# First batch of a gated block: carries tile by tile, diag(D) on VectorE, y to x2 interleaved, GpSimd pausing

## The chip, the cores and the metric

The kernel runs on one core of a Trainium2 chip. The metric is the device time of one execution in microseconds (us), the median of three runs. The engines are named as in the profile: PE is TensorE (matrix products and transposes), PEld its weight loads, DVE is VectorE, ACT is ScalarE, POOL is GpSimd, SP is the engine that only issues DMAs here.

## The reference

Four batches of 512 rows by 512 columns go through two parts. The first is a state space model (Mamba) over a context of 256 columns, gated by the normalised input; the second is a mixture of experts with one shared and seven routed experts.

```python
def _ssm_forward(hidden_states, z, in_proj_w, conv_w, conv_b, x_proj_w, dt_proj_w, dt_proj_b, A_log, D):
    x = jnp.einsum('ed,bld->bel', in_proj_w, hidden_states)
    ...
    u = jax.nn.silu(xc + conv_b[None, :, None])          # xc: causal convolution of x, 4 taps
    x_dbl = jnp.einsum('ke,bel->bkl', x_proj_w, u)       # dt_lo, Bm, Cm
    delta = jax.nn.softplus(jnp.einsum('er,brl->bel', dt_proj_w, dt_lo) + dt_proj_b[None, :, None])
    # scan over l, 16 states:  state = state * exp(delta * A) + (delta * u) * Bm ;  y = sum_n state * Cm
    y = y + D[None, :, None] * u
    y = y * jax.nn.silu(z)
    return jnp.swapaxes(y, 1, 2)

x = x + jnp.tanh(g_xattn[0]) * ssm(ctx, layernorm(x))
x = x + jnp.tanh(g_ffn[0]) * moe(layernorm(x))           # silu(x@W1) * (x@Wg) @ W2, 1 shared + top 3 of 7
```

## The kernel before

A batch is four tiles of 128 rows or channels by 512 (T = 4). The products of the experts are made in three passes from a high and a low half of each operand (`x_hi`, `x_lo`, `w_split`, `h_hi`, `h_lo`), 12 products of 128x512 for one bank.

Each engine has its own program, written out by hand in its order; the engines meet at semaphores. There is no planner: what stands earlier in an engine's program is done earlier, and an instruction that waits holds up all behind it on that engine.

The first batch's state space part is done by itself, since there are no expert products yet to lie beside it:

- **The front.** The context is projected (`in_proj`), convolved (`first_conv`), and `xproj` gives `dt_x` and `xdbl`. The softplus of delta is built on ACT and DVE: ACT reads the product of a tile twice and takes an exponential (`front_dt`, three instructions per tile into `dA[0]` and `delta`), and later the logarithm into `st[0]` (`front_ln`). DVE computes the rounding error of 1 + e in three instructions per tile (`front_carry`: L1238, L1241, L1246, all in `st[1]` and `delta`), and adds the logarithm (`front_delta`, L1253). Then it makes delta times u (`front_du`, L1264), which also waits until PE has used `u` for the term D u (`first_init`, L589, which reads `diag_D`, four diagonal matrices). POOL normalises the input of z in place meanwhile (L1668).
- **The scans.** For each of 16 states DVE multiplies (`bmul`, L1275) and scans (`scan`, L1284), two instructions each; PE transposes the states into rows, ACT scales them by C, PE adds them into four PSUM banks (`first_add`, L596). PE also projects the contexts of the later batches in halves (`in_proj`, L550), and ACT stages them to memory (`stage`).
- **From y to x2.** DVE makes y from bank and gate (`first_make_y`, L1337), adds the residual (L1353), takes the statistics (L1356), and `first_mean_and_var` and `first_x2` (L1331) make the normalised x2. POOL makes the low halves of the shared expert's three matrices here (`first_low`, L1596, four instructions for each matrix) and the two powers for the norm (`first_power`, L1588). PE makes 20 products that nobody reads, to keep its clock up (`keep_warm`, L533), and then transposes x2 (`x2_to_columns`, L631); ACT makes `x_hi` from it and DVE `x_lo`.
- **The shared expert of batch 0** (`shared_step`), with the front of batch 1 laid between its products at numbered places g (PE), j (ACT) and p (DVE). DVE does 8 instructions of the convolution of batch 1 (L1179) before the first `h_tmp` (L1444) and 4 behind it. ACT's `front_silu` (L858) waits for these, and behind it stands ACT's `router_columns` (L984), which PE's `router_rows` waits for at g = 3.

Of the kernel before, what the change touches and what calls it, by code (L numbers as in the profile page):

```python
# [28 lines left out]
def gated_block(nc, t, out):  # L29
# [22 lines left out]
    with ExitStack() as ctx:  # L52
# [88 lines left out]
        setup_a = sem("setup_a")  # L141
        ctx_ld = sem("ctx_ld")
# [380 lines left out]
        def _(pe):  # L523
# [212 lines left out]
            def shared_step(b, m=None):  # L736

                def between(g):
                    if g == 1:
                        router_columns(b)  # L740
                    if g == 3:
                        router_rows(b)
                    if m is not None:
                        names = {5: ("xproj", "init0"), 6: ("dt0", "init1"), 7: ("dt1", "ccols"), 8: ("dt2", "init2"),
                                 9: ("dt3", "init3"), 10: ("z0", "z1")}.get(g, ())
                        front(m, *[name for name in names if name in front_names(m)])
# [38 lines left out]
            pe.wait_ge(setup_a, 2 + T)  # L785
# [6 lines left out]
            for n in range(DS):  # L792
# [9 lines left out]
                in_proj(2 + q // T, q % T, (n % 2,))  # L802
# [17 lines left out]
        def _(act):  # L820
# [311 lines left out]
            for et in range(T):  # L1132
                act.activation(diag_D[:, et, :], ident[:], ACT.Copy, scale=D_col[:, et:et + 1]).then_inc(setup_a, 1)
            for et in range(T):
                front_dt(0, et)
            front_ccols(0)
            front_ln(0, range(T))
# [7 lines left out]
            for n in range(DS):  # L1145
                decays(0, T * (n + 2), T * (n + 2) + 2)
                for i in range(T):
                    first_scale(n, i)
# [4 lines left out]
                if n % 2:  # L1153
                    stage(2 + q // T, q % T)
                if n == DS - 2:
# [14 lines left out]
        def _(dve):  # L1170
# [176 lines left out]

            def residual(m, tiles):

                dve.wait_ge(xres_ld, 16 * (m + 1))  # L1350
                for i in tiles:
                    dve.wait_ge(y_ready, T * m + i + 1)
                    dve.tensor_tensor(x1[:, i, :], y_rows[:, i, :], x_rows[:, i, :], ALU.add).then_inc(x1_ready, 1)  # L1353
                for i in tiles:
                    dve.wait_ge(x1_ready, T * m + i + 1)
                    dve.bn_stats(bn[:, i, :], x1[:, i, :]).then_inc(x2stat, 1)  # L1356
# [121 lines left out]
            front_carry(0, (0, 1))  # L1478
            front_carry(0, (2, 3))
# [15 lines left out]
            for h in range(2):  # L1495
                for i in (2 * h, 2 * h + 1):
                    first_make_y(i)
                    residual(0, (i,))
                first_mean_and_var(h)
# [80 lines left out]
        def _(pool):  # L1580
# [91 lines left out]
            first_low(1, (0, 1))  # L1672
            first_power(0)
            first_low(1, (2,))
            first_power(1)
            first_low(1, (3,))
# [43 lines left out]
```

## Time and profile before

| | us |
|---|---|
| median of 3 runs | 1354.61 (1353.84 to 1354.89) |
| profiled execution, its own time | 1356.03 |
| its span in the profile | 1354.2 |
| PE busy | 1307.6 (97%) |
| DVE busy | 963.6 (71%) |
| ACT busy | 622.5 (46%) |
| POOL busy | 613.8 (45%) |

The profile is of one execution. In the page's 40 slices PE stands at 9 tenths or more except in the first, the second and the fifth (7, 8 and 7 tenths; a slice is 33.9 us). PE's mean granted clock over the execution is 0.991 of 2.4 GHz. Times are counted from the start of the span. The row of a merged group gives its start, the time to the end of its last instruction, and the number of instructions (x4); fp32 products show as two records each.

### The profile page before, as it was taken

The page shows a single profiled execution, that of the slowest core. Times are in us where ns is not written, and L with a number is a line of the kernel's source. Part 1 is how long each engine was busy: PE and PEld are TensorE (multiplying, and loading weights), DVE is VectorE, ACT ScalarE, POOL GpSimd, SP SyncE. Part 2 cuts the span into 40 slices and gives each one's busy share as a digit, 9 for nine tenths or more (in the row PEclk, how much of TensorE's full clock was granted, in tenths as well). Part 3 has the DMA queues.
Part 4 walks back from the last instruction along what each step waited for, and adds up shares of the span by engine and source line. Part 5 has one row for each costly group of instructions (what it writes and reads, how often), then busy time and mean ns, then how long its engine had stood idle before and what let it go on. Part 6 is the DMA issues. An engine that isn't in the chain of part 4 may idle for free.

```text
span 1354.2 us, 17537 instructions
## 1 busy us (share of the span) xinstructions
PE 1307.6 (97%) x5986; PEld 1032.5 (76%) x5986; DVE 963.6 (71%) x1062; ACT 622.5 (46%) x1016; POOL 613.8 (45%) x337
## 2 busy tenths in 40 slices
PE   7899799999999999999999999999999999999999
PEld 4455478787777787888887878888887888888887
DVE  6999867899999776699999776699999623111111
ACT  6888466665565336544454135555444121111111
POOL 3000545788898521467667511566767411111111
PEclk8999899999999999999999999999999999999999
DMA  6211676776667755555566755655555665555552
GB/s 224 78 63 55 228 285 248 270 260 234 222 251 272 286 201 192 197 171 174 196 210 210 278 189 202 202 190 184 176 183 189 218 218 187 186 186 186 186 191 88
DMA packets 92588, 269.69 MB, mean 199 GB/s; under 512 B 11664, under 2 KB 11792, under 8 KB 92128
## 3 DMA queue, kind: packets, MB, share of 16 engines
q1 hardware_dynamic: 87200, 261.54, 55.9%
q10 hardware_dynamic: 5312, 7.16, 1.5%
q8 instruction: 45, 0.74, 0.2%
q14 instruction: 31, 0.25, 0.1%
HBM read 210.73 MB, written 57.93 MB: 198 GB/s over the span
## 4 chain that ended last, share of the span: by engine, by line
PE 80%; DVE 13%; issue 4%; ACT 2%; DMA 0%; DVEq 0%; POOL 0%; ACTq 0%
PE ps_hg L527 24%; PE ps_h L527 21%; PE ps_y L527 15%; PE ps_y L708 8%; DVE st L1284 7%; PE ps_mid L606 5%; DVE y_rows L1295 1%; DVE st L1275 1%; PE ps_h L596 1%; PE ps_mid L568 1%; ACT dA L937 1%; PE ps_y L550 1%; PE ps_mid L527 1%; PE ps_hg L596 1%; PE ps_y L596 1%
## 5 line engine op out<-in xcount | busy, mean ns | idle before, releaser
L1606 POOL TENSOR_TENSOR h_lo<-h_tmp,h_hi 128x512 fp32r<-128x512 f32 x128 | 237.1, 1856 | 478.2 <-ACT h_hi L1012 415.8
L527 PE MATMUL ps_h<-x_hi,w_split 128*128 128x512 f32 x1024 | 344.9, 399 | 1.1 <-ACT x_hi L974 0.9
L527 PE MATMUL ps_hg<-x_hi,wg_split 128*128 128x512 f32 x1024 | 342.8, 396 | 0.6 <-DVE h_tmp L1444 0.6
L1284 DVE TENSOR_TENSOR_SCAN st<-dA,st 128x1024 f32<-128x1024 f32 x128 | 326.9, 2564 | 0.0
L1444 DVE TENSOR_TENSOR h_tmp<-h_tmp,ps_hg 128x512 f32<-128x512 f32 x128 | 88.0, 688 | 267.1 <-PE ps_hg L527 264.6
L527 PE MATMUL ps_y<-w_split,h_hi 128*128 128x512 f32 x1024 | 254.1, 395 | 0.0
L1012 ACT ACTIVATE h_hi<-h_tmp 128x512 fp32r<-128x512 f32 x128 | 80.7, 630 | 328.9 <-DVE h_tmp L1444 328.9
L527 PEld LDWEIGHTS ps_h<-x_hi,w_split 128*128 128x128 f32 x1024 | 193.2, 189 | 42.4 <-issue 2.5
L527 PEld LDWEIGHTS ps_hg<-x_hi,wg_split 128*128 128x128 f32 x1024 | 192.4, 188 | 40.6 <-issue 1.0
L527 PEld LDWEIGHTS ps_y<-w_split,h_hi 128*128 128x128 f32 x1024 | 188.5, 188 | 37.9
L1006 ACT ACTIVATE h_tmp<-ps_h 128x512 f32<-128x512 f32 x128 | 76.2, 595 | 283.1 <-PE ps_h L527 280.1
L527 PE MATMUL ps_hg<-x_lo,wg_split 128*128 128x512 f32 x512 | 199.5, 390 | 0.0
L527 PE MATMUL ps_h<-x_lo,w_split 128*128 128x512 f32 x508 | 197.9, 390 | 0.0
L1275 DVE TENSOR_TENSOR st<-u,b_all 128x1024 f32<-128x1024 f32 x128 | 188.2, 1480 | 0.1
L937 ACT ACTIVATE dA<-delta,neg_A 128x511 f32<-128x511 f32 x256 | 162.8, 708 | 5.6 <-DVE dA L1225 2.8
L606 PEld LDWEIGHTS ps_mid<-ident,st 128*128 128x128 f32 x748 | 90.0, 140 | 58.2 <-DVE st L1284 21.4
L708 PE MATMUL ps_y<-w_split,h_lo 128*128 128x512 f32 x512 | 134.3, 393 | 0.0
L606 PE MATMUL ps_mid<-ident,st 128*128 128x128 f32 x748 | 112.0, 275 | 20.8 <-DVE st L1284 20.8
L1437 DVE SCALAR_TENSOR_TENSOR acc<-ps_y,coef,acc 128x512 f32<-128x512 f32 x112 | 82.5, 737 | 69.5 <-PE ps_y L708 69.5
L1627 POOL TENSOR_TENSOR st<-st,wg_raw 128x512 f32<-128x512 f32 x48 | 96.4, 2031 | 47.1 <-DVE st L1284 47.1
L527 PEld LDWEIGHTS ps_hg<-x_lo,wg_split 128*128 128x128 f32 x512 | 96.5, 188 | 18.7
L708 PEld LDWEIGHTS ps_y<-w_split,h_lo 128*128 128x128 f32 x512 | 94.6, 188 | 20.8 <-POOL h_lo L1606 1.7
(163 smaller groups left out, 1329.0 us busy)
## 6 DMA issues: line engine op xcount, KB each, us to landing
w_split<-split_scratch SPq DMA_DIRECT2D x192, 512.0 KB, 5.2
wg_split<-split_scratch SPq DMA_DIRECT2D x96, 512.0 KB, 4.6
split_scratch<-w_split SPq DMA_DIRECT2D x64, 512.0 KB, 4.3
b_all<-xd_scratch SPq DMA_DIRECT2D x64, 256.0 KB, 4.1
split_scratch<-wg_split SPq DMA_DIRECT2D x32, 512.0 KB, 3.1
w_raw<-in_W_dram SPq DMA_DIRECT2D x14, 1024.0 KB, 8.1
wg_raw<-in_Wg_dram SPq DMA_DIRECT2D x7, 1024.0 KB, 9.5
dA<-in_x_dram SPq DMA_DIRECT2D x4, 1024.0 KB, 7.4
```

Source lines behind the costliest of these rows:

```text
L527: mm = pe.matmul(out_, lhs[a], rhs[c], start=first and q == 0, stop=last and q == len(sides) - 1)
L606: mm = pe.transpose(ps_mid[bank][:, et * P:(et + 1) * P], st[n % 2][:, et, i * P:(i + 1) * P], ident[:])
L708: mm = pe.matmul(ps_y[i % 3][:], h_lo[:, j, i * P:(i + 1) * P], half(2, j, 0), start=False, stop=j == T - 1)
L937: act.activation(dA[odd][:, et, 1:L], delta[:, et, 1:L], ACT.Exp, scale=neg_A[:, et, n:n + 1]).then_inc(da_ready, 1)
L1006: act.activation(h_tmp[j % 2][:], ps_h1[j % 2][:], ACT.Silu).then_inc(t_done, 1)
L1012: act.activation(h_hi[:, j, :], h_tmp[j % 2][:], ACT.Copy).then_inc(hh_ready, 1)
L1275: dve.tensor_tensor(st[odd][:, two], u[:, two], b_all[odd][:].rearrange("p (a l) -> p a l", a=1).broadcast_to([P, 2, L]), ALU.mult).then_i ...
L1284: dve.tensor_tensor_scan(flat[1], flat[0], flat[1], 0.0, ALU.mult, ALU.add).then_inc(scan_done, 1)
L1437: dve.scalar_tensor_tensor(out=acc[:, i, :], in0=ps_y[i % 3][:], scalar=scale, in1=before[:, i, :], op0=ALU.mult, op1=ALU.add).then_inc(ac ...
L1444: dve.tensor_tensor(h_tmp[j % 2][:], h_tmp[j % 2][:], ps_hg[:], ALU.mult).then_inc(h_made, 1)
L1606: pool.tensor_tensor(h_lo[:, j, :], h_tmp[j % 2][:], h_hi[:, j, :].bitcast(F32), ALU.subtract).then_inc(hl_ready, 1)
L1627: pool.tensor_tensor(st[odd][:, et, :], st[odd][:, et, :], c_all[used % 2], ALU.mult).then_inc(col_scaled, 1)
```

## The change

Seven edits, all in the first batch or in the shared step beside it:

1. `diag_D` is made by DVE (four instructions, before the carries) in place of ACT; PE waits for a semaphore of its own (`diag_made`).
2. `front_carry` of batch 0 is done tile by tile in place of pair by pair.
3. ACT does `front_ln` of batch 0 ahead of `front_ccols`.
4. The last half of `in_proj` for batch 3 goes from state 15 to state 14, where the last tile is now projected in one piece; its staging on ACT goes with it, to before the fourth scaling of state 14. The load of ACT's table for Silu goes to the end of state 13.
5. On DVE, y, residual and statistics of the tiles are interleaved, so that most instructions have another one between them and the one that they depend on.
6. POOL does no low halves between the first matrix (`first_low(0)`) and the end of x2: it does the two powers and then waits for all four tiles of x2.
7. In the shared step of batch 0, PE transposes the columns of C for batch 1 (`ccols`, L579) behind the first half of the down products (g = 8) in place of before it (g = 7).

The 20 warming products stay as they are.

```diff
@@ shared_step (PE)
+                        if not late(m):
+                            names = {7: ("dt1",), 8: ("ccols", "dt2", "init2")}.get(g, names)
                         front(m, *[name for name in names if name in front_names(m)])
@@ tensor
-            pe.wait_ge(setup_a, 2 + T)
+            pe.wait_ge(diag_made, T)
...
-                in_proj(2 + q // T, q % T, (n % 2,))
+                if n < DS - 2:
+                    in_proj(2 + q // T, q % T, (n % 2,))
+                elif n == DS - 2:
+                    in_proj(2 + q // T, q % T)
@@ scalar
-            for et in range(T):
-                act.activation(diag_D[:, et, :], ident[:], ACT.Copy, scale=D_col[:, et:et + 1]).then_inc(setup_a, 1)
             for et in range(T):
                 front_dt(0, et)
+            front_ln(0, range(T))
             front_ccols(0)
-            front_ln(0, range(T))
...
+                    if n == DS - 2 and i == T - 1:
+                        stage(NB - 1, T - 1)
                     first_scale(n, i)
...
-                if n % 2:
+                if n % 2 and n < DS - 2:
                     stage(2 + q // T, q % T)
+                if n == DS - 3:
+                    table(ACT.Silu)
@@ vector
-            front_carry(0, (0, 1))
-            front_carry(0, (2, 3))
+            for et in range(T):
+                dve.tensor_scalar(diag_D[:, et, :], ident[:], D_col[:, et:et + 1], None, ALU.mult).then_inc(diag_made, 1)
+            for et in range(T):
+                front_carry(0, (et,))
...
             for h in range(2):
-                for i in (2 * h, 2 * h + 1):
-                    first_make_y(i)
-                    residual(0, (i,))
-                first_mean_and_var(h)
+                first_make_y(2 * h)
+                if h:
+                    first_mean_and_var(0)
+                residual_add(0, 2 * h)
+                first_make_y(2 * h + 1)
+                residual_stats(0, 2 * h)
+                residual_add(0, 2 * h + 1)
+                residual_stats(0, 2 * h + 1)
+            first_mean_and_var(1)
@@ gpsimd
             first_low(0, range(T))
-            first_low(1, (0, 1))
             first_power(0)
-            first_low(1, (2,))
             first_power(1)
-            first_low(1, (3,))
+            pool.wait_ge(x2_ready, T)
+            first_low(1, range(T))
             first_low(2, range(T))
```

How the instructions stand, first on DVE at the front of batch 0. Before, where `st` and `dA` are the buffers of 1 + e and e, and `delta` takes the correction:

```order
L1476 TENSOR_SCALAR neg_A<-neg_A 128x64
L1238 TENSOR_SCALAR st<-dA 128x512 x2
L1241 SCALAR_TENSOR_TENSOR st<-st,dA 128x512 x2
L1246 TENSOR_TENSOR delta<-delta,st 128x512 x2
L1238 TENSOR_SCALAR st<-dA 128x512 x2
```

And after:

```order
L1491 TENSOR_SCALAR neg_A<-neg_A 128x64
L1494 TENSOR_SCALAR diag_D<-ident,D_col 128x128 x4
L1246 TENSOR_SCALAR st<-dA 128x512
L1249 SCALAR_TENSOR_TENSOR st<-st,dA 128x512
L1254 TENSOR_TENSOR delta<-delta,st 128x512
L1246 TENSOR_SCALAR st<-dA 128x512
```

Four small instructions stand ahead of the carries, and a tile's three instructions follow each other.

POOL between the z of batch 0 (`dA`) and the low half of the shared step's first `h_tmp`, before. `w_split` stands for the first matrix at the top and the third lower down, `wg_split` for the second, `rstd` for the powers:

```order
L1668 TENSOR_SCALAR dA<-dA,mv,rstd 128x512 x4
L1596 TENSOR_TENSOR w_split<-w_raw,w_split 128x512 x4
L1596 TENSOR_TENSOR wg_split<-wg_raw,wg_split 128x512 x2
L1588 TENSOR_TENSOR rstd<-var_eps,minus_half 128x2
L1596 TENSOR_TENSOR wg_split<-wg_raw,wg_split 128x512
L1588 TENSOR_TENSOR rstd<-var_eps,minus_half 128x2
L1596 TENSOR_TENSOR wg_split<-wg_raw,wg_split 128x512
L1596 TENSOR_TENSOR w_split<-w_raw,w_split 128x512 x4
L1601 TENSOR_TENSOR w_split<-w_raw,w_split 128x512
L1606 TENSOR_TENSOR h_lo<-h_tmp,h_hi 128x512
```

And after:

```order
L1690 TENSOR_SCALAR dA<-dA,mv,rstd 128x512 x4
L1618 TENSOR_TENSOR w_split<-w_raw,w_split 128x512 x4
L1610 TENSOR_TENSOR rstd<-var_eps,minus_half 128x2 x2
L1618 TENSOR_TENSOR wg_split<-wg_raw,wg_split 128x512 x4
L1618 TENSOR_TENSOR w_split<-w_raw,w_split 128x512 x4
L1623 TENSOR_TENSOR w_split<-w_raw,w_split 128x512
L1628 TENSOR_TENSOR h_lo<-h_tmp,h_hi 128x512
```

All eight low halves of the second and third matrix now stand behind both powers; before, three stood ahead of the second power.

PE at the end of the shared step's gate products, before (`dt_x` is batch 1's dt product, `xdbl` its C columns, `h_hi` the down products):

```order
L575 MATMUL ps_mid<-dt_x,dt_w 128x512
L579 MATMUL ps_mid<-ident,xdbl 128x128 x4
L527 MATMUL ps_y<-w_split,h_hi 128x512 x16
L575 MATMUL ps_mid<-dt_x,dt_w 128x512
L572 MATMUL ps_mid<-ident,st 128x128 x4
```

And after:

```order
L576 MATMUL ps_mid<-dt_x,dt_w 128x512
L528 MATMUL ps_y<-w_split,h_hi 128x512 x16
L580 MATMUL ps_mid<-ident,xdbl 128x128 x4
L576 MATMUL ps_mid<-dt_x,dt_w 128x512
L573 MATMUL ps_mid<-ident,st 128x128 x4
```

The four transposes, which wait until ACT has read a bank, have gone behind 16 products that don't.

## Rows read from the trace of the kernel before

**Rows 1.** Busy time in stretches: us, each engine, PEclk, DMA share, GB/s.

```profile
38.90:145.20 106.30, 97.65 (x402) 54.86 (x402) 106.29 (x65) 89.28 (x150) 0.00 (x0) 0.98 0.24 82
145.20:166.90 21.70, 15.04 (x62) 10.24 (x63) 17.41 (x28) 7.15 (x13) 15.76 (x13) 0.82 0.64 226
182.60:1354.20 1171.60, 1149.01 (x5369) 937.24 (x5366) 801.22 (x907) 491.67 (x798) 579.77 (x311) 1.00 0.60 207
```

**Rows 2.** The timeline of ACT at the front: start us, us, instruction, count.

```profile
22.59 1.26 ACT L1133 ACTIVATE diag_D<-ident,D_col 128x128 f32<-128x128 f32 x4
23.76 0.67 ACT L916 ACTIVATE dA<-ps_mid,dt_b 128x512 f32<-128x512 f32 x1
...
29.88 0.66 ACT L919 ACTIVATE dA<-dA 128x512 f32<-128x512 f32 x1
...
31.96 2.56 ACT L928 ACTIVATE st<-dA,ones 128x512 f32<-128x512 f32 x4
```

**Rows 3.** The timeline of DVE at the front.

```profile
23.47 0.19 DVE L1476 TENSOR_SCALAR neg_A<-neg_A 128x64 f32<-128x64 f32 x1
25.62 0.43 DVE L1238 TENSOR_SCALAR st<-dA 128x512 f32<-128x512 f32 x1 [1.97 <-ACT dA L919]
...
31.06 1.28 DVE L1241 SCALAR_TENSOR_TENSOR st<-st,dA 128x512 f32<-128x512 f32 x2
...
33.47 2.90 DVE L1253 TENSOR_TENSOR delta<-delta,st 128x512 f32<-128x512 f32 x4
...
36.51 2.29 DVE L1264 TENSOR_TENSOR u<-delta,u 128x2048 f32<-128x2048 f32 x1
```

**Rows 4.** The timeline of POOL at the front.

```profile
24.54 10.79 POOL L1668 TENSOR_SCALAR dA<-dA,mv,rstd 128x512 f32<-128x512 f32 x4
```

**Rows 5.** The timeline of PE at the front.

```profile
33.56 1.06 PE L589 MATMUL ps_y<-diag_D,u 128*128 128x128 f32 x8
```

**Rows 6.** The timeline of PE at the end of the scans.

```profile
146.61 1.02 PE L550 MATMUL ps_y<-acc,in_w 128*128 128x512 f32 x2
147.47 1.02 PE L596 MATMUL ps_h<-y_rows,ident 128*128 128x512 f32 x2
...
150.95 5.15 PE L533 MATMUL ps_y<-gw 128*128 128x512 f32 x20
```

**Rows 7.** The timeline of DVE from y to x2.

```profile
149.47 1.32 DVE L1353 TENSOR_TENSOR z<-y_rows,delta 128x512 f32<-128x512 f32 x1
...
159.02 0.69 DVE L1353 TENSOR_TENSOR z<-y_rows,delta 128x512 f32<-128x512 f32 x1
...
160.84 4.02 DVE L1331 TENSOR_SCALAR st<-z,mv,rstd 128x512 f32<-128x512 f32 x4
```

**Rows 8.** The timeline of POOL from the last scan on.

```profile
145.28 4.96 POOL L1596 TENSOR_TENSOR w_split<-w_raw,w_split 128x512 fp32r<-128x512 f32 x4 [109.95 <-DVE st L1284]
```

**Rows 9.** Busy time in the stretch between the warming products and x2.

```profile
156.10:161.40 5.30, 0.00 (x0) 0.00 (x0) 5.05 (x11) 0.00 (x0) 1.28 (x2) 0.76 0.89 290
```

**Rows 10.** The chain that ended last, at the first expert products: start us, us, what.

```profile
166.92 3.75 PE ps_h L527 x8
...
177.15 2.75 PE ps_h L527 x12
```

**Rows 11.** The timeline of DVE, the convolution of batch 1.

```profile
167.40 6.24 DVE L1179 SCALAR_TENSOR_TENSOR u<-dA,conv_w,u 128x509 f32<-128x509 f32 x8
...
176.00 4.82 DVE L1179 SCALAR_TENSOR_TENSOR u<-dA,conv_w,u 128x511 f32<-128x511 f32 x4
```

**Rows 12.** The timeline of POOL beside it.

```profile
178.52 1.75 POOL L1612 TENSOR_TENSOR wg_split<-wg_raw,wg_split 128x512 fp32r<-128x512 f32 x1
```

**Rows 13.** The timeline of ACT, the router's columns.

```profile
181.39 0.57 ACT L984 ACTIVATE xdbl<-ps_mid 14x512 f32<-14x512 f32 x1
```

**Rows 14.** Waits of PE from 182 us on: waited for, us in total, times, longest.

```profile
PE ps_mid L606 <- DVE st L1284: 17.3, 21, 1.7
PE ps_mid L579 <- ACT y_rows L893: 1.1, 1, 1.1
```

More of the change, by code:

```diff
@@ L141, in gated_block @@
         setup_a = sem("setup_a")
+        diag_made = sem("diag_made")
         ctx_ld = sem("ctx_ld")
@@ L1346, in make_y, with residual_add, residual_stats @@
                                              in1=z2[:, i, :], op0=ALU.mult, op1=ALU.mult).then_inc(y_ready, 1)
+            def residual_add(m, i):
+                dve.wait_ge(xres_ld, 16 * (m + 1))
+                dve.wait_ge(y_ready, T * m + i + 1)
+                dve.tensor_tensor(x1[:, i, :], y_rows[:, i, :], x_rows[:, i, :], ALU.add).then_inc(x1_ready, 1)
+            def residual_stats(m, i):
+                dve.wait_ge(x1_ready, T * m + i + 1)
+                dve.bn_stats(bn[:, i, :], x1[:, i, :]).then_inc(x2stat, 1)
             def residual(m, tiles):
-                dve.wait_ge(xres_ld, 16 * (m + 1))
                 for i in tiles:
-                    dve.wait_ge(y_ready, T * m + i + 1)
-                    dve.tensor_tensor(x1[:, i, :], y_rows[:, i, :], x_rows[:, i, :], ALU.add).then_inc(x1_ready, 1)
+                    residual_add(m, i)
                 for i in tiles:
-                    dve.wait_ge(x1_ready, T * m + i + 1)
-                    dve.bn_stats(bn[:, i, :], x1[:, i, :]).then_inc(x2stat, 1)
+                    residual_stats(m, i)
             def make_x2(m):
```

## The prediction

> **What bounds the kernel now.** I first read the table of stretches, to see which engine carries which part. The reader is to see three stages. In the scans of batch 0, DVE is busy for 106.29 of 106.30 us [rows 1]: whatever lets them start earlier ends them earlier by as much. From the last scan to the first expert product, 21.7 us, no engine is full: DVE has 17.41, POOL 15.76, PE 15.04, and this is a chain through DVE. From 182.6 us on PE is busy for 1149.0 of 1171.6 us [rows 1], and DVE, which waits for PE in each step, follows it, so a gain made before is kept to the end; the 17.3 us in 21 waits for scans [rows 14] move along with it. The change touches only the first 210 us. Then I read the timelines of each engine there: the front up to 36.5 us, the way from y to x2, and the first expert step.
>
> **The front, edits 1 to 3.** Before, ACT makes diag_D from 22.59 and begins the first tile's dt at 23.76 [rows 2]; without it, all that follows on ACT comes 1.17 earlier, and the last e is ready at 30.54 - 1.17 = 29.4. The tiles' e come 1.66 apart (the fourth exponential starts at 29.88, the first at 23.76 + 0.57 + 0.57), the first is ready at 24.4. With `front_ln` ahead of `ccols` (about 0.25) the logarithms gain that too: they end at 34.52 - 1.42 = 33.1.
>
> DVE gets four 128x128 instructions behind neg_A, which ends at 23.66 [rows 3]. The trace has no such instruction; the nearest row is neg_A itself, half as wide, 0.19, and the other end is the 128x512 of the same kind, 0.43. I take 0.19 each, so 0.76 and the carries may start at 24.4, just when the first e is there; with 0.43 each they would start at 25.4, one us late. Then each tile takes 0.43 + 0.04 for the first instruction, 0.64 + 0.08 for the second because its result is waited for, and 0.60 for the third (1.28 for two, from rows 3): 1.79. DVE is a little slower than ACT's 1.66, so the fourth tile's carries end at 24.4 + 3 x 1.79 + 0.47 + 0.72 + 0.60 = 31.6, where before they ended at 33.47 [rows 3]. The four additions take 2.4 and the clearing of one column 0.8 with its wait, so delta u starts at 34.2 in place of 36.51. In the trace two instructions beside POOL's normalisation took 0.4 longer than their kind (the four additions 2.90 in place of 2.5 [rows 3]); since DVE has no slack now, both count, and I take 0.6 for them: 34.8, a gain of **1.7**. The ends are 1.0 (0.43 for each diag, and clashes as well) and 2.3 (neither). What might be late next: PE's term D u, which ended at 34.6 [rows 5], is moved with ACT's reading of the banks (1.17 earlier) and is at 33.4 to 34.5, so it just does not bind; z of batch 0 comes from POOL (done at 35.33, [rows 4]) and is wanted by the second state, some 8 us later.
>
> This is a place to weigh a page. The rows show DVE's TENSOR_SCALAR of 0.43 at 25.62 in the midst of POOL's four TENSOR_SCALARs of 2.7 each (10.79 / 4) [rows 3, 4], not held up by them. The Trainium skill (SBUF — State Buffer, Who interferes with whom) says that a VectorE instruction in a two-port mode, which tensor_scalar can take, and a GpSimd one exclude each other for a whole instruction. By that the four diag instructions or the first carry would wait for POOL's power or first tile; the trace disagrees for this pair of instructions. It is the fourth rival below.
>
> **State 14 and 15, edit 4.** At state 15 the half projection (0.86, from 146.61 to 147.47, [rows 6]) goes from ahead of the first sum. At state 14 the same 0.86 comes in; PE is not quite full there (97.65 of 106.30 in the scans, [rows 1]), and I estimate that about half of it is hidden and the rest pushes the transposes of state 15: the first sum starts at 147.05 in place of 147.47. So y of tile 0 comes 0.4 earlier. The table load of 1.28 on ACT is in ACT's gaps in either place. But then the residual (L1353) of tile 0, which took 1.32 from 149.47 where the free one takes 0.69 [rows 7], ended when POOL's fourth low half (4 in 4.96 from 145.28, so to 150.24, [rows 8]) had ended, plus 0.55. That does not move: **0** from edit 4, unless DVE asks before POOL's fourth one starts at 149.0 (I have DVE at 149.05); the third rival.
>
> **From y to x2, edits 5 and 6.** The other residuals pay the same clash: it is one POOL instruction, then one of DVE, in turn. Interleaved and with POOL silent, I lay the sequence out from 150.8: y1, statistics 0, add 1, statistics 1 (0.66, 0.61, then 0.73 where the next depends), y2 at 153.4, mean and variance 0.37, add 2 at 154.5, y3, statistics 2, add 3 at 156.3, statistics 3, variance, x2 from 158.2 against 160.84 [rows 7]. The second power takes about 0.9 after that, and the last two x2 at 0.43 end at 160.1; before, the four took 4.02 [rows 7] and ended at 164.86. So x2 is ready 4.8 us earlier. PE's transposes then follow at 158.7, after 3.1 us of idleness; before it was 5.3, and the clock went from 1.0 to 0.5 within (mean 0.76) [rows 9]. I take it that it falls again; then PE needs to 162.6 for the transposes, and the first product starts at 163.4 in place of 166.92 [rows 10].
>
> **What that gives back.** POOL now has eight low halves to do from 160.15, at 1.23 each, and the first weight split of the next step behind them; before, five were left at 161.9 and they were nearly through when DVE's convolution of batch 1 began at 167.40. That first one waited, the other seven went at 0.66 [rows 11]. Now it begins at 163.9, with one of POOL's eight under way and four to come, and the split behind them. Both read two tensors from SBUF, so they take turns: in the second convolution group four took 4.82 against two POOL instructions of 1.75 [rows 11, 12], which is 1.19 for POOL's and 0.55 for DVE's, 1.74 a pair. The first ends at 165.6, the sixth at 174.3, the eighth at 175.6; `h_tmp` of the first tile comes at 175.65, where it was 175.39. Behind it the four of the last tap meet the same two POOL instructions as before, then ACT's silu, then `router_columns`: read to the end at 182.2 (before 181.96, [rows 13]). PE's `router_rows` then starts at 182.25 in place of 182.65. Of 3.5 us that PE was earlier, only **0.4** is left, and PE stands idle for 3 us from 179.2. The bounds: -1.5 (pairs at 2.0, below) and 3.5 (no turns).
>
> The Trainium skill (the same page and section) gives the same rule, an exclusive lock between a VectorE op with two SBUF inputs and a GpSimd op that reads SBUF; it speaks against edit 6, since pausing only moves the low halves into the convolution. Here the trace agrees (0.69 free, 1.32 beside POOL).
>
> **Edit 7.** PE waited 1.1 us at g = 7 for ACT to read a bank [rows 14]. Behind 16 products the bank has long been read. ACT's reading of the columns comes at about the time that ACT gets there anyway, but PE's second init transposes may wait some 0.25 for it. Gain **0.85**, between 0.5 and 1.1.
>
> **The sum.** 1.7 + 0 + 0.4 + 0.85 = 2.95 us. The profiled execution took 1356.03 (span 1354.2 and 1.8 around it), and would take 1353.1; the median of the runs is 1.4 lower, 1354.61, and I predict 1351.7 for it.
>
> **Rivals.**
> - *The clock falls a second time.* In the 3 us before `router_rows` (and perhaps before the second gate products) PE does nothing; before, 5.3 us of that took the clock down from 1.0 (2.4 GHz) to 0.5 (1.2 GHz) [rows 9]. Then the next products run at 1.2 GHz: 8 took 3.75 where 12 take 2.75 [rows 10], so 0.24 lost on each; ten of them give 2.4. Time: 1351.7 + 2.4 = 1354.1. For it: the idle stretch is as long as the one ahead of x2. Against it: PE is full on both sides of it. The Trainium skill (TensorE: Matmul & The Clock Gate, the section on the HAM clock gate) says that the count of slow products differs from run to run of one kernel; no run here shows it.
> - *The backlog costs more than it brings.* If DVE and POOL take turns at their full lengths (1.27 and 0.74, 2.0 a pair in place of 1.74), the eight convolution instructions end 2.1 later, `router_rows` at 184.4 in place of 182.65: 1.8 lost in place of 0.4 gained. PE then idles for 5 us, so the clock falls too, 2.9 (the 12 products of a bank at half speed). -1.7 + 1.8 + 2.9 - 0.85 = 2.1 slower: 1356.7, and 1357.4 with the front at its low end. It decides when `h_tmp` of the first tile comes behind 177. Against it: the pairs of 1.74 in rows 11 and 12.
> - *DVE gets ahead of POOL's fourth low half.* Then the residual of tile 0 ends 1.2 earlier, x2 and all the turns with it: 1350.5. It takes 0.1 us.
> - *The diag instructions are blocked by POOL.* The carries would start when the first of POOL's 2.7 us has ended, 27.3 in place of 24.4, and lose 2.8: 1354.5. Against it, rows 3 and 4.
> - *The convolution doesn't take turns with the low halves.* Then all 3.5 us are kept: 1351.7 - 3.1 = 1348.6. Against it, rows 11.
>
> **Chances.** The forecast 0.42; the second fall of the clock 0.22; the costly backlog 0.10; DVE ahead 0.12; diag blocked 0.06; no turns 0.08. What a measurement of this kernel can tell from no change is 0.2%, 2.7 us, so faster means under 1351.9. The forecast lies just at it, and about six tenths of it is beyond; with the third and the fifth rival and a little of the first this makes 0.47 faster, 0.43 the same, 0.10 slower. The range is 1349.4 to 1356.0: it leaves out most of the fifth rival and of the second.
>
> **What would show it.** Delta u at 34.8 (34.2 to 35.5), and the last scan's end at about 143.5. The last x2 near 158.4 (4.8 before its old place, and 1.7 on top), the first convolution instructions at 1.7 us each beside POOL, the first `h_tmp` later than the end of its gate products, and a wait of PE of about 3 us at `router_rows`. No wait at L580 for an `init` bank. I am wrong if the convolution goes at 0.66 each, if PE has no such wait, or if the scans start less than 1 us earlier. A clock of 0.5 behind `router_rows` shows the first rival.

## The result and the profile after

The changed kernel takes 1357.85 us (median of 15 runs, 1356.61 to 1359.72), the kernel before in the same rounds 1355.47 (15 runs). The ratio is 1.0020, 95% interval 1.0014 to 1.0027: 2.7 us slower by the ratio, where 3 us faster was forecast. The profiled execution took 1359.72 (span 1357.9), 3.69 us of span more than the one before; it was the slowest of the 15, so part of what this profile shows is not in the median.

The front, ACT. Columns: start us, us, instruction, count.

```profile
22.65 0.26 ACT L1137 ACTIVATE neg_A<-neg_A 128x64 f32<-128x64 f32 x1
22.84 0.69 ACT L922 ACTIVATE dA<-ps_mid,dt_b 128x512 f32<-128x512 f32 x1
...
30.95 2.56 ACT L934 ACTIVATE st<-dA,ones 128x512 f32<-128x512 f32 x4
```

DVE beside it, with the first tile's three carry instructions in full, and POOL's normalisation of z:

```profile
23.91 0.87 DVE L1494 TENSOR_SCALAR diag_D<-ident,D_col 128x128 f32<-128x128 f32 x4
24.70 0.42 DVE L1246 TENSOR_SCALAR st<-dA 128x512 f32<-128x512 f32 x1
25.15 1.14 DVE L1249 SCALAR_TENSOR_TENSOR st<-st,dA 128x512 f32<-128x512 f32 x1
26.33 0.69 DVE L1254 TENSOR_TENSOR delta<-delta,st 128x512 f32<-128x512 f32 x1
...
33.66 2.49 DVE L1261 TENSOR_TENSOR delta<-delta,st 128x512 f32<-128x512 f32 x4
...
36.29 2.29 DVE L1272 TENSOR_TENSOR u<-delta,u 128x2048 f32<-128x2048 f32 x1
...
24.75 9.03 POOL L1690 TENSOR_SCALAR dA<-dA,mv,rstd 128x512 f32<-128x512 f32 x4
```

Against [rows 2 to 4]: ACT is earlier as forecast (22.84 for 23.76, and the logarithms 30.95 for 31.96), diag_D costs 0.8. But delta u has gained only 0.22 us, 36.29 for 36.51. The second carry instruction takes 1.14 where its kind took 0.68, in each of the four tiles, and the carries end only at 33.7. When the front begins differs from execution to execution by up to 1 us. So delta u is better counted from ACT's instruction on `neg_A` just ahead of the front, at 22.65 here; before it stood at 22.43:

```profile
22.43 0.26 ACT L1131 ACTIVATE neg_A<-neg_A 128x64 f32<-128x64 f32 x1
```

From there to delta u it is 14.08 us before and 13.64 after, a gain of 0.44. All seven profiles with the old front have 14.07 or 14.08 there, all nine with edits 1 to 3 and POOL as before 13.64 or 13.65.

From x2 to the first hidden tile, DVE, then POOL:

```profile
157.75 2.13 DVE L1339 TENSOR_SCALAR st<-z,mv,rstd 128x512 f32<-128x512 f32 x4
...
162.82 12.26 DVE L1187 SCALAR_TENSOR_TENSOR u<-dA,conv_w,u 128x509 f32<-128x509 f32 x8
175.00 0.68 DVE L1459 TENSOR_TENSOR h_tmp<-h_tmp,ps_hg 128x512 f32<-128x512 f32 x1
...
159.96 5.42 POOL L1618 TENSOR_TENSOR wg_split<-wg_raw,wg_split 128x512 fp32r<-128x512 f32 x4 [1.12 <-DVE st L1339]
165.35 6.82 POOL L1618 TENSOR_TENSOR w_split<-w_raw,w_split 128x512 fp32r<-128x512 f32 x4
172.13 1.73 POOL L1623 TENSOR_TENSOR w_split<-w_raw,w_split 128x512 fp32r<-128x512 f32 x1
```

PE there; in brackets the idle time before a group and what ended it:

```profile
158.35 1.36 PE L632 MATMUL ps_mid<-ident,st 128*128 128x128 f32 x8 [2.84 <-DVE st L1339]
162.34 3.72 PE L528 MATMUL ps_h<-x_hi,w_split 128*128 128x512 f32 x8 [0.89 <-ACT x_hi L980]
175.82 0.47 PE L528 MATMUL ps_hg<-x_hi,wg_split 128*128 128x512 f32 x1 [1.50 <-DVE h_tmp L1459]
181.57 0.66 PE L649 MATMUL ps_mid<-ident,xdbl 128*128 128x128 f32 x4 [2.75 <-ACT xdbl L990]
```

Here the forecast was right in detail: x2 ends 5.0 us earlier (159.88), the first product starts at 162.34 for 166.92 [rows 10], the convolution takes 12.26 us in turns with POOL in place of 6.24 [rows 11], and of the 4.6 us PE has 0.9 left at `router_rows` (181.57 for 182.46), behind a wait of 2.75. In the same stretch, and again much later, the clock falls. The columns are the engines' busy us, then PEclk:

```profile
183.00:186.40 3.40, 3.40 (x9) 2.63 (x8) 3.32 (x10) 1.01 (x3) 3.37 (x3) 0.50 1.03 422
1029.50:1032.90 3.40, 3.40 (x11) 2.81 (x10) 1.78 (x1) 0.00 (x0) 3.40 (x3) 0.50 0.31 120
```

0.50 is 1.2 GHz; PE was full and made about half as many products (9 and 11 records for the 17 and 20 of the kernel before). Just before the later one stands what no part of the forecast spoke of. DVE, POOL and PE at that place, after (of POOL's pair the merged row, then the second instruction by itself):

```profile
1025.09 0.69 DVE L1459 TENSOR_TENSOR h_tmp<-h_tmp,ps_hg 128x512 f32<-128x512 f32 x1 [1.79 <-PE ps_hg L528]
1025.70 3.43 DVE L1292 TENSOR_TENSOR_SCAN st<-dA,st 128x1024 f32<-128x1024 f32 x1
...
1024.44 2.54 POOL L1649 TENSOR_TENSOR st<-st,wg_raw 128x512 f32<-128x512 f32 x2
...
1025.69 1.29 POOL L1649 TENSOR_TENSOR st<-st,wg_raw 128x512 f32<-128x512 f32 x1
...
1026.94 5.48 POOL L1655 TENSOR_TENSOR w_raw<-w_raw,st 128x512 f32<-128x512 f32 x2
...
1029.26 0.95 PE L607 MATMUL ps_mid<-ident,st 128*128 128x128 f32 x4 [1.91 <-DVE st L1292]
```

And before:

```profile
1023.89 0.69 DVE L1444 TENSOR_TENSOR h_tmp<-h_tmp,ps_hg 128x512 f32<-128x512 f32 x1 [1.44 <-PE ps_hg L527]
1024.49 2.53 DVE L1284 TENSOR_TENSOR_SCAN st<-dA,st 128x1024 f32<-128x1024 f32 x1
...
1023.59 4.52 POOL L1627 TENSOR_TENSOR st<-st,wg_raw 128x512 f32<-128x512 f32 x2
...
1024.83 3.27 POOL L1627 TENSOR_TENSOR st<-st,wg_raw 128x512 f32<-128x512 f32 x1
...
1027.15 0.65 PE L606 MATMUL ps_mid<-ident,st 128*128 128x128 f32 x4 [0.65 <-DVE st L1284]
```

DVE's `h_tmp` begins 0.35 us later against the product that it waits for (1.79 for 1.44). So the order of the next two turns is another. After, POOL's second instruction starts at 1025.69, just ahead of the scan, and takes 1.29, and the scan takes 3.43 in place of 2.53. Before, the scan was first, and POOL's second took 3.27. PE waits 1.91 in place of 0.65.

**The stages, in twelve of the eighteen profiles.** Read off the same instructions in each trace (us): scans = delta u to the last scan's end; y-x2 = to the end of the last x2; h_tmp = to the first `h_tmp`; rows = to `router_rows`; 249 = to a split on ACT at 248.4 us of before; loop = to the first product of the next batch (788.5); state = to the `h_tmp` of 1023.9; turn = to a `bmul` on DVE 17 us behind it. What follows took 313.03 to 313.05 in every profile.

| | delta u | scans | y-x2 | h_tmp | rows | 249 | loop | state | turn |
|---|---|---|---|---|---|---|---|---|---|
| before | 36.51 | 108.68 | 19.67 | 10.53 | 7.07 | 65.96 | 540.08 | 235.39 | 17.32 |
| after | 36.29 | 108.69 | 14.90 | 15.12 | 6.57 | 66.84 | 540.92 | 235.77 | 19.79 |
| after, again | 36.12 | 109.65 | 14.89 | 15.10 | 6.58 | 65.27 | 540.41 | 235.73 | 18.21 |
| edits 1-3 | 36.59 | 108.88 | 18.54 | 10.22 | 7.06 | 65.97 | 540.02 | 235.39 | 17.32 |
| edit 7 | 37.47 | 108.95 | 18.55 | 10.25 | 7.07 | 65.23 | 540.30 | 235.40 | 17.32 |
| edit 5 | 36.96 | 109.64 | 18.41 | 9.80 | 7.07 | 65.96 | 540.59 | 235.41 | 17.31 |
| edit 6 | 37.24 | 109.66 | 15.89 | 15.13 | 6.58 | 66.03 | 540.22 | 235.36 | 17.32 |
| edits 5, 6 | 37.19 | 109.66 | 14.92 | 15.12 | 6.57 | 66.03 | 540.46 | 235.41 | 17.32 |
| all but 6 | 36.75 | 108.70 | 18.42 | 10.53 | 7.07 | 65.25 | 540.46 | 235.76 | 19.81 |
| all, one wait | 36.69 | 109.03 | 14.88 | 14.91 | 6.58 | 65.31 | 540.07 | 235.40 | 17.33 |
| all but 6, one wait | 36.67 | 108.70 | 18.40 | 10.51 | 7.07 | 65.26 | 540.02 | 235.35 | 17.32 |
| waits alone | 36.48 | 108.68 | 18.54 | 9.74 | 6.83 | 65.97 | 540.06 | 235.75 | 18.22 |

Read down a column: most have a few values only. "scans" is 108.7 to 109.0 or 109.65, and "loop" is 540.0 to 540.9, in one kernel as in another: chance of the execution. y-x2 is 18.4 to 18.6 in the eleven other profiles without the pause, and only the one profile that I had read shows 19.67: it was 1.1 us slow just there. It was slow in the next stage as well. There DVE waited 1.75 us for PE, whose clock was at 0.50 until 172.6 us. With the waits alone the clock was back at 169.2, DVE didn't wait, and h_tmp is 9.74 for 10.53. The row of before comes first, then that of the waits alone (columns as above, then DMA share and GB/s):

```profile
158.95:172.55 13.60, 9.83 (x29) 7.46 (x30) 13.24 (x21) 5.34 (x9) 7.46 (x6) 0.50 1.01 369
158.95:169.15 10.20, 7.59 (x24) 5.74 (x25) 9.94 (x17) 5.21 (x8) 7.47 (x6) 0.50 1.02 381
```

### The profile page after: what moved, and what is told of

It is laid out like the page before. It is cut to its first block, busy times and chain, and to the rows that moved or that the text cites. A ratio compares the mean times of both kernels' runs of the same rounds, so it can differ in the third digit from the quotient of the medians.

```text
span 1357.9 us, 17544 instructions
## 1 busy us (share of the span) xinstructions
PE 1309.5 (96%) x5986; PEld 1034.7 (76%) x5986; DVE 968.3 (71%) x1066; ACT 621.1 (46%) x1013; POOL 614.2 (45%) x337
## 4 chain that ended last, share of the span: by engine, by line
PE 79%; DVE 14%; issue 4%; ACT 2%; DMA 0%; DVEq 0%; ACTq 0%
PE ps_hg L528 24%; PE ps_h L528 21%; PE ps_y L528 15%; PE ps_y L709 8%; DVE st L1292 7%; PE ps_mid L607 5%; PE ps_h L597 1%; DVE y_rows L1303 1%; DVE u L1187 1%; DVE st L1283 1%; PE ps_mid L569 1%; ACT dA L943 1%; PE ps_y L551 1%; PE ps_y L597 1%; PE ps_hg L597 1%
## 5 line engine op out<-in xcount | busy, mean ns | idle before, releaser
L528 PEld LDWEIGHTS ps_h<-x_lo,w_split 128*128 128x128 f32 x508 | 95.9, 189 | 19.1 <-issue 0.5
```

Source lines behind the costliest of these rows:

```text
L528: mm = pe.matmul(out_, lhs[a], rhs[c], start=first and q == 0, stop=last and q == len(sides) - 1)
```

## The experiments

A ratio is against the kernel before, which ran beside each (27 to 33 runs, medians 1355.3 to 1355.4); 0.0001 is 0.14 us. Each ratio is known to about 0.0009, 1.2 us.

**1. Edits 1 to 3 alone.** The diff is those three edits of the change.

> Edits 1 to 3 alone (diag_D on DVE, carries tile by tile, logarithms before ccols); all the rest as before. Theory A (the loss comes from y to x2 and the pause): the front's 0.2 to 0.4 us show at delta u (36.1 to 36.3), router_rows keeps its place less 0.3, the clock stays up at 183, and the time is that of the kernel before, -0.5 to +0.3 us. Theory B (any shift of the first 200 us re-times the turns of DVE and POOL in batches 1 to 3, and that costs): +1 to +3 us, with the difference arising behind 788 us as in the changed kernel.

Measured: 1355.23, ratio 0.9998 (0.9989 to 1.0007). L1240 takes 1.14 in each tile. Delta u at 36.59 is later than expected, because this execution began its front late; from `neg_A` it is 13.64 for 14.08. Nothing was lost behind 788 us: Theory A, and the front is worth 0.4 us, which the times can't tell from nothing.

**2. Edits 5 and 6 alone.**

> Edits 5 and 6 alone (y, residual and statistics interleaved; POOL makes no low halves until all of x2 is there). Theory A: x2 5 us earlier, router_rows 0 to 0.5 us earlier with a wait of PE of 2.5 to 3 us, the clock at 0.5 behind it (+1.5 us at the first product of the next bank), and about +1 to +2.5 us in all. Theory B: the time depends on the shift alone, +1 to +3 us with the difference behind 788 us; if x2's way costs nothing at 183 us it is this one.

Measured: 1357.15, ratio 1.0010 (1.0001 to 1.0019). x2 and the backlog as in the changed kernel (14.92 + 15.12), PE waits 2.76 at `router_rows`, but the clock did not fall behind it in this profile. A gain was forecast for these edits; they lose 1.4 us, between 0.1 and 2.6.

**3. Edit 7 alone.**

> Edit 7 alone (ccols at g = 8). Theory A: -0.3 us from 204 us on, absorbed at the gate product of step 1 (h_tmp of tile 3 comes from DVE at its old time), so 0.0 +- 0.3 us. Theory B: +1 to +3 us if already this shift re-times the later batches. If neither, -0.85 us as the prediction had it.

Measured: 1354.41, ratio 0.9991 (0.9982 to 1.0000). The stage "249" is 65.23 for 65.96, and the gain stays to the end: near the forecast's 0.85, and neither A nor B. All profiles with edit 7 in which the clock doesn't fall there have 65.2 to 65.3, those without it 66.0.

**4. All edits but 6.**

```diff
-            first_power(0)
-            first_power(1)
-            pool.wait_ge(x2_ready, T)
-            first_low(1, range(T))
+            first_low(1, (0, 1))
+            first_power(0)
+            first_low(1, (2,))
+            first_power(1)
+            first_low(1, (3,))
```

> The changed kernel without edit 6: POOL makes the low halves of the second and third matrix between the powers as before. Theory A (the pause is what costs): x2 about 2.5 us later than with the pause, but the convolution of batch 1 untouched by turns, h_tmp of the first tile 1 to 3 us earlier than 175.0, PE full before router_rows, the clock up; -0.5 to -2 us against before. Theory B: +1 to +3 us like the changed kernel.

Measured: 1356.66 (1355.13 to 1357.58), ratio 1.0006 (0.9997 to 1.0015). PE is full before `router_rows`, and up to 788 us this profile is 1.3 us ahead of before (y-x2, where that one was slow, alone makes 1.25: 18.42 for 19.67). Then come the wait of 1.91 at 1027 and the clock's fall behind it, and 2.9 us are lost (state and turn, 255.57 for 252.71). So the late loss hangs neither on the pause nor, by experiments 1 to 3, on a mere shift of time: Theory B falls as well.

**5. Edit 5 alone, and 6. edit 6 alone.**

> Edit 5 alone: y, residual and statistics interleaved, POOL makes its low halves between the powers as before. Theory P (the pause alone costs, since eight low halves take turns with the convolution of batch 1): x2 at most 1 us earlier, h_tmp of the first tile at 174.3 to 175.4, PE full before router_rows, time -0.6 to +0.3 us against before. Theory I (the interleaving itself re-times turns and costs): +1 us or more.

> Edit 6 alone: POOL pauses until all of x2 is there, DVE's order from y to x2 as before. Theory P: x2 3 to 4 us earlier, the first expert product too, h_tmp of the first tile no earlier than 175, a wait of PE of 2 to 3 us before router_rows, time +1.2 to +2 us. Theory I: within 0.5 us of before.

Measured: interleaving 1355.11, ratio 1.0001 (0.9992 to 1.0010); the pause 1358.33, ratio 1.0022 (1.0013 to 1.0031). Theory P: the pause makes y to x2 2.65 us shorter (15.89 for 18.54) and the way to `h_tmp` 4.9 us longer (15.13 for 10.25). But its time is a miss: 3.0 us were lost where Theory P had 1.2 to 2. Alone the pause costs more than together with the interleaving (1.4 in experiment 2), and the traces show why in part. With POOL silent the interleaving takes 1.0 us off y to x2 (14.9 for 15.9); beside POOL's low halves it takes 0.14 (18.41 for 18.55).

**7. Edits 1, 2, 3 and 7.**

> Edits 1, 2, 3 and 7, the parts that gained or cost nothing by themselves. Theory 1 (the gains add): -0.2 - 1.0 = -1.2 us, so about 1354.2. Theory 2 (edit 7's gain and the front's are the same wait at the gate product of step 1 and don't add, or the late turn at 1027 us goes the other way): 0 to -0.5 us, or +1 with the clock's fall at 1030.

Measured: 1354.33, ratio 0.9993 (0.9984 to 1.0002). The gains add within what is measured, Theory 1; by the interval Theory 2's 0 to -0.5 isn't excluded.

**8. The changed kernel again.**

> The changed kernel once more, unaltered: a second profile. Theory S (systematic): the pause ahead of the first product behind batch 1's last step (0.99 us of issue at 788 us in place of 0.26) and the scan of 3.43 us at 1025.7 us with the clock's fall at 1030 come again. Theory C (chance): the profile shows 0.26 or 0.62 and a PE wait of 0.65 at 1027 us, a span near 1354.9, and still 1 us or more lost by 200 us. Median 1357.9 +- 0.5 in both.

Measured: 1357.54, ratio 1.0021 (1.0011 to 1.0030), span 1355.0. The wait at 1027 is there, the two falls of the clock are not:

```profile
1028.00:1031.40 3.40, 3.40 (x19) 2.85 (x20) 1.94 (x1) 0.00 (x0) 3.40 (x3) 1.00 0.30 113
183.70:187.10 3.40, 3.40 (x17) 2.78 (x16) 3.32 (x10) 2.37 (x6) 3.40 (x3) 1.00 1.02 418
```

So the wait is of the kernel, the falls are of the execution, 1.6 us each (66.84 for 65.27, and 19.79 for 18.21). The Trainium skill (TensorE: Matmul & The Clock Gate, the section on the HAM clock gate) says that the count of slow products differs between runs of one kernel. These two profiles agree: 9 records in 3.4 us at 183 us in one, 17 in the other.

What the two kernels with the late wait (three profiles) had in common was the length of DVE's program: its trace has 1661 instructions, waits counted. Before it has 1652, with edit 5 alone 1658, with edits 1 to 3 alone 1655. (The expectations below count the compiled program, which for 1661 in the trace gives 1525.) Edit 5 repeats the wait for x's rows for every tile, in the later batches too, and some of these waits are instructions of their own. That gave Theory F.

**9. Only more waits, at the front.**

```diff
             dve.wait_ge(setup_v, 4)
+            for _ in range(13):
+                dve.wait_ge(setup_v, 4)
```

> The kernel before with 13 more waits on DVE for a semaphore that has long been reached, ahead of the first carry; six more instructions in DVE's program, and no other work. Theory F (where DVE's program stalls by 0.35 us is set by how many instructions stand before that place): DVE's h_tmp of 1023.9 us waits 1.79 in place of 1.44, POOL's column products go before the scan, PE waits 1.9 at 1027 in place of 0.65, and the time is +1.2 us, or +4 where the clock falls at 1030. Theory E (it is what edits 4 and 5 do to the first batch that shifts the later ones): gap 1.44 and PE wait 0.65, 0.0 +- 0.3 us.

Measured: 1355.77, ratio 1.0002 (0.9993 to 1.0011), gap 1.43 and PE wait 0.65. Six more instructions ahead of everything don't do it. This kernel is then as long as that with edit 5 alone, 1658 instructions, and in neither is any such instruction late from 188 us on.

**10. The changed kernel with one wait per residual.**

```diff
             def residual_add(m, i):
-                dve.wait_ge(xres_ld, 16 * (m + 1))
...
             def residual(m, tiles):
+                dve.wait_ge(xres_ld, 16 * (m + 1))
...
+            dve.wait_ge(xres_ld, 16)
             for h in range(2):
                 first_make_y(2 * h)
```

> The changed kernel, but with the wait for the rows of x once per residual and not once per tile (ten instructions fewer in DVE's program); no work changed. Theory F: h_tmp of 1023.9 waits 1.44 again, PE 0.65 at 1027, no fall of the clock there, and the time is 1.2 to 2.5 us below the changed kernel: 1355.3 to 1356.4. Theory E: as the changed kernel, 1357.7.

Measured: 1355.35 (1355.04 to 1356.91), ratio 1.0003 (0.9994 to 1.0012), 2.2 us below the changed kernel (1356.81 to 1359.09), with no work changed. The place at 1027 is as before:

```profile
1022.87 0.69 DVE L1459 TENSOR_TENSOR h_tmp<-h_tmp,ps_hg 128x512 f32<-128x512 f32 x1 [1.44 <-PE ps_hg L528]
1023.48 2.53 DVE L1292 TENSOR_TENSOR_SCAN st<-dA,st 128x1024 f32<-128x1024 f32 x1
...
1026.14 0.65 PE L607 MATMUL ps_mid<-ident,st 128*128 128x128 f32 x4 [0.65 <-DVE st L1292]
```

The 0.35 us have gone to the `h_tmp` at 349.82 (a wait of 1.77 for 1.44 before), where nothing follows from them. In this profile PE waited 3.46 us ahead of the first tile's second gate products, and the clock fell in that wait; in experiment 6 it fell a second time at 178.4 (this kernel's row first, then experiment 6's):

```profile
174.90:181.70 6.80, 5.37 (x12) 3.80 (x12) 5.99 (x6) 3.60 (x7) 3.56 (x3) 0.50 1.04 397
178.45:181.80 3.35, 3.06 (x7) 2.48 (x8) 3.35 (x5) 2.35 (x5) 2.46 (x2) 0.50 1.03 370
```

Neither cost time: PE's wait at `router_rows` was shorter instead (0.29 and 1.34 in place of 2.75), and `router_rows` came 6.58 us behind `h_tmp` as in the others with the pause.

**11. The same without the pause.**

> The same without edit 6: edits 1 to 5 and 7, the wait for x's rows once. Theory F: 1.1 to 1.8 us below the former, 1353.7 to 1354.5, the fastest of these kernels. Theory E: as with the repeated waits, 1356.7.

Measured: 1354.02 (1353.59 to 1354.50), ratio 0.9992 (0.9983 to 1.0001). Against experiment 10, all of whose runs lie above all of these, this is the price of the pause with the interleaving, 1.3 us. Of it the two profiles show 0.4 between the last scan and `router_rows` (36.36 for 35.98); where the rest lies is not shown. With experiment 15 it is the fastest version here, 3.5 us below the changed kernel and 1.3 below before (at the edge of its interval).

**12. POOL's normalisation of z behind the carries**, with edits 1 to 3.

```diff
             pool.wait_ge(zrstd, 1)
+            pool.wait_ge(carry3, T)
```

> Edits 1 to 3, and POOL begins the normalisation of z only when DVE has made the carries. Theory L (the 1.14 us of each tile's second carry instruction is a turn with POOL): it takes 0.68, a tile 1.79 in place of 2.24, the carries end 1.8 us earlier, and delta u starts 1.3 to 1.8 us earlier than with edits 1 to 3 alone; the scans end earlier by as much. Theory D (it is the wait for the instruction just before): 1.14 again, and delta u where it was. The end is -1 to -1.5 us against before by L, -0.2 by D.

Measured: 1366.08, ratio 1.0081 (1.0067 to 1.0095). The front of this kernel on DVE:

```profile
24.45 0.42 DVE L1237 TENSOR_SCALAR st<-dA 128x512 f32<-128x512 f32 x1
24.90 0.69 DVE L1240 SCALAR_TENSOR_TENSOR st<-st,dA 128x512 f32<-128x512 f32 x1
25.62 0.69 DVE L1245 TENSOR_TENSOR delta<-delta,st 128x512 f32<-128x512 f32 x1
26.23 0.42 DVE L1237 TENSOR_SCALAR st<-dA 128x512 f32<-128x512 f32 x1
...
34.64 2.29 DVE L1263 TENSOR_TENSOR u<-delta,u 128x2048 f32<-128x2048 f32 x1
```

The mechanism of L is shown: 0.69, a tile in 1.78, delta u at 34.64. Its time is a miss: POOL's four instructions now stood beside DVE's full stream and took 16.07 us for 9.03, the normalised input came at 47.9, and DVE waited 11.6 us, until 55.8, for the z that is made from it.

**13. The waits alone**, in the order of the kernel before.

```diff
-                dve.wait_ge(xres_ld, 16 * (m + 1))
                 for i in tiles:
+                    dve.wait_ge(xres_ld, 16 * (m + 1))
                     dve.wait_ge(y_ready, T * m + i + 1)
...
             dve.wait_ge(setup_v, 4)
+            for _ in range(7):
+                dve.wait_ge(setup_v, 4)
```

> The kernel before with the wait for x's rows repeated for every tile of a residual, as edit 5 has it, and 7 more waits for a reached semaphore ahead of the carries, so that DVE's program is as long as the changed kernel's (1525 instructions) and stands alike from the middle of batch 0 on; no work is moved. Theory F: h_tmp of 1023.9 us waits 1.79 in place of 1.44, PE 1.9 at 1027, time +1.25 us, and up to +4 where the clock falls at 1030: a median of 1356.6 to 1357.9. Theory E: gap 1.44, time within 0.5 us of before.

Measured: 1356.70 (1355.10 to 1357.73), ratio 1.0011 (1.0002 to 1.0020): 1.5 us slower, between 0.3 and 2.7. DVE and PE of this kernel:

```profile
1022.05 0.69 DVE L1444 TENSOR_TENSOR h_tmp<-h_tmp,ps_hg 128x512 f32<-128x512 f32 x1 [1.79 <-PE ps_hg L527]
1022.66 3.43 DVE L1284 TENSOR_TENSOR_SCAN st<-dA,st 128x1024 f32<-128x1024 f32 x1
...
1026.22 0.65 PE L606 MATMUL ps_mid<-ident,st 128*128 128x128 f32 x4 [1.91 <-DVE st L1284]
```

With no work moved, the stall, the turned order and PE's wait are there. Theory F holds for this kernel, whose program has the changed kernel's length (1661) and its repeated waits.

**14. Carries by pairs** (experiment 11 with edit 2 undone), **15. without edit 4** (experiment 11 with the half projection at state 15).

> Edits 1, 3, 4, 5 and 7, with the wait for x's rows once; without the pause and with the carries pair by pair as before. If the tile-by-tile carries lose what the earlier start brings (each pays 0.45 us for its turn with POOL, with ACT's e no longer what they wait for), pairs are better: delta u at 35.4 to 35.8 in place of 36.6, and 1353.0 to 1353.6 against 1354.0 with edit 2. If not, delta u at 36.5 and 1354.0.

> Edits 1, 2, 3, 5 and 7, with the wait for x's rows once: no pause, and the half projection at state 15 as before. If edit 4 is worth nothing, as forecast, 1354.0 +- 0.4 us and x2 ready 18.4 us after the last scan as with it; else 1354.4 or more, with x2 0.4 later.

Measured: pairs 1354.24, ratio 0.9993 (0.9984 to 1.0002), from the first carry to delta u 11.71 us for 11.59 by tiles: the two orders are worth the same. The turns with POOL only move. No second carry instruction is held up in this profile (0.68 each), but four others are, by 0.41 each. Without edit 4 1354.01, ratio 0.9991 (0.9982 to 1.0000), y-x2 18.40 as with it: edit 4 is worth 0, as forecast.

**16. A pause only until the second power**, all else as in experiment 10.

```diff
             first_power(1)
-            pool.wait_ge(x2_ready, T)
             first_low(1, range(T))
```

> All seven edits with the wait for x's rows once, but POOL pauses only until the second power, not until x2 is ready. If what the pause costs is the backlog beside the convolution, the low halves begin 2 us earlier, the first h_tmp comes at 173.5 to 174.3 in place of 175.5, and the time is that without the pause, 1353.7 to 1354.3; if x2's own instructions take turns with POOL, x2 is 2 us later and the time is 1354.5 to 1355.4.

Measured: 1356.10 (1353.82 to 1356.80), ratio 1.0006 (0.9997 to 1.0015). The third of the four x2, with POOL's first low half at 159.71:

```profile
159.77 1.49 DVE L1339 TENSOR_SCALAR st<-z,mv,rstd 128x512 f32<-128x512 f32 x1
```

The free ones take 0.54. x2 takes turns too, y-x2 is 16.79 for 14.88, and nothing is won; the median is 0.7 above the end of what was expected for this case.

## Why the prediction was wrong, by its own steps

- **The front, 1.7 us forecast, 0.44 measured in the traces (0.3 in the time of experiment 1). This step failed first, by the size of one term.** The prediction had seen two DVE instructions held up by 0.4 beside POOL and took 0.6 for all. Tile by tile, one instruction in each of the four tiles pays 0.46, 1.8 in all; experiment 12 takes POOL away and gets the forecast's 1.79 per tile and its 34.8 (34.64). The prediction's reason, that DVE "has no slack now", is not what the runs show. In experiment 14 DVE waits for the second e as long as before (1.20 for 1.17), and yet four instructions are held up where two were. What differs there is when POOL begins its four against the first carry: 1.08 us ahead of it before, 0.05 behind it in experiment 14. That this decides how many clash was not tested. (In the sum of the front, "0.8" for clearing a column doesn't fit: 31.6 + 2.4 + 0.8 is 34.8 and not 34.2. The trace before has 0.15 there, and with that 34.2 stands.)
- **Diag on DVE: right.** 0.87 us for four (0.2 each), nothing blocked, though POOL's power was under way (to 24.65). The fourth rival did not come. (Its 2.7 us for POOL's first instruction is the mean of four that took 2.08, 2.08, 3.18 and 3.50.)
- **Edit 4, 0: right** (experiment 15). y of tile 0 came 0.36 earlier against the last scan in this profile (not in experiment 8's), and the residual waited for POOL's fourth low half as before. DVE asked 0.14 us after that one had started, so the third rival missed by little.
- **Edits 5 and 6, -0.4 forecast, +1.4 measured (experiment 2).** Every mechanism was right, the turns of 1.7 us a pair included, and against the profile in hand the size too: from the last scan to `router_rows` 36.6 for 37.3 (the 182.65 that it gives for `router_rows` before is 182.46 in the trace). But that profile is not the kernel. Its 19.67 us from the last scan to x2 are 18.4 to 18.6 in the others without the pause, and its way on to `h_tmp` was at the slow end too. Against those eleven the stretch is 36.6 for 34.9 to 36.0. A gain of 0.4 was taken as a difference of two numbers of 5 us, one of them from a single profile of turns that fall one way or the other.
- **Edit 7, 0.85: right** (0.73 in the stage, ratio 0.9991 alone, so 0 to 2.4).
- **"A gain made before 182.6 is kept to the end": right for work, wrong for the program.** Nothing between 249 and 1023 us takes back or adds what came before (columns "loop" and "state"), apart from chance of up to 0.9. But edit 5's repeated waits changed DVE's program in the later batches, and by that one turn at 1024 us: 0.37 and 0.9 us in each of the four profiles that have it, 1.6 more where the clock falls behind it (in two of the four, and in none of the fourteen others). Experiments 10 and 13 show it from both sides: 2.2 us less and 1.5 more with no work moved. This is the largest single term, and no step of the prediction had it: it put what repeated waits do at nothing, without a reason.
- **The first rival** (the clock falls a second time) came in one of the two profiles of the changed kernel, at 183 us, and cost 1.6 where 2.4 was given. In experiments 6 and 10 it fell earlier in the same stretch and cost nothing, since PE had its wait at `router_rows` to spare.
- **The second rival** (the costly backlog) had the time, 1356.7 to 1357.4 on the forecast's scale, where 1354.61 x 1.0020 is 1357.3, but not the reason. By its own sign `h_tmp` would have come behind 177 and `router_rows` at 184.4; they came at 175.00 and 181.57. That the numbers meet is chance.

The terms by the medians: front and edit 7 together -1.0 (experiment 7), edits 4 and 5 without their waits -0.3 (experiment 11 against 7, less than can be told), the pause +1.3 (10 against 11), the repeated waits +2.2 (8 against 10): 2.2 slower. Each term is the difference of two of these kernels in a row, so that they add up to experiment 8's 2.2 is no check on them. The first measurement has 2.4 by the medians.

Left open: what makes the 0.35 us. The runs show that its place goes with the length of DVE's program; whether the length itself decides, or where the waits stand in it, and what in the chip it comes from, is not shown. Which of two values the scans take (108.7 or 109.65) is open as well.

## What to carry to other kernels

Where two engines take turns, a price read from one profile is one throw: look at the same stretch in a second profile of the same kernel before setting a gain of 0.4 us against it, and don't count on as many clashes as the old trace has once one of the two starts at another moment. Work that is moved out of the way goes somewhere; moving POOL's eight instructions from y to x2 into the convolution cost more than it gave. And a helper that is rewritten for one place is rewritten for all its callers: look at the length of each engine's program before and after, also where the work is the same. To compare one stage in two profiles, count from an event of the same execution just ahead of it and not from the start of the span.

## What the runs showed that was not expected

- DVE starts one or two instructions some 0.35 us late, and in all eighteen profiles the places (read from 188 us on, by the time of the profile before) go with the number of DVE's instructions in the trace. With 1652 it is 532 us (380 ns of idle before batch 2's delta u, 7 to 11 in the others), with 1655 (edits 1 to 3) it is 238 and 1129 (a wait of 0.66 for 0.31), with 1661 (the changed kernel, experiments 4 and 13) 238 and 1024, with 1651 (experiments 10, 11, 14 to 16) 350, with 1658 (edit 5 alone, edits 5 and 6, experiment 9) none was seen.
- TENSOR_SCALAR on DVE beside POOL: mostly 0.42 with POOL's TENSOR_SCALAR under way (front), once 0.83 (at 29.97 before), and 1.49 for 0.54 beside POOL's TENSOR_TENSOR (experiment 16). The prediction set the rule of the Trainium skill (SBUF — State Buffer, Who interferes with whom), an exclusive lock for a whole instruction, against the front's rows. The second pair behaves by it; the first does not, since even the one that was held up was held up by 0.41 us only, where POOL's instruction beside it took 3.18.
- The first product of the next batch starts 0.17 to 0.99 us after PE could, by no wait that the profile shows, and differently in two profiles of the same kernel (0.99 and 0.58).
